# A four-stage scan on VectorE: the first stage's base built from the net term and a slope that holds q, the base and the clamp of p placed anew, and the wait for the base put ahead of the wait for TensorE

## What is computed

```python
def _derivative(q, p, drive, coupling, bias):
    i_couple = jnp.tanh(q) @ coupling.T
    dq = q - q ** 3 / 3.0 - p + drive + i_couple + bias
    dp = EPSILON * (q + ALPHA - BETA * p)
    return (dq, dp)

def _rk4_step(q, p, drive, coupling, bias):
    dq1, dp1 = _derivative(q, p, drive, coupling, bias)
    dq2, dp2 = _derivative(q + 0.5 * DT * dq1, p + 0.5 * DT * dp1, drive, coupling, bias)
    dq3, dp3 = _derivative(q + 0.5 * DT * dq2, p + 0.5 * DT * dp2, drive, coupling, bias)
    dq4, dp4 = _derivative(q + DT * dq3, p + DT * dp3, drive, coupling, bias)
    q_next = q + DT / 6.0 * (dq1 + 2 * dq2 + 2 * dq3 + dq4)
    p_next = p + DT / 6.0 * (dp1 + 2 * dp2 + 2 * dp3 + dp4)
    return (jnp.clip(q_next, -CLAMP, CLAMP), jnp.clip(p_next, -CLAMP, CLAMP))
```

## Time and profile before

| what | value |
|---|---|
| median of 3 runs (lowest, highest) | 5519.89 us (5515.1, 5520.47) |
| the profiled execution: its own time / its span | 5520.96 us / 5519.1 us |
| VectorE busy, share of the span | 4193.2 us, 76% |
| TensorE matmuls busy, share of the span | 4445.0 us, 81% |
| ScalarE / GpSimd busy | 2313.8 us, 42% / 1737.6 us, 31% |
| the scan's 4096 `result` instructions | start from 49.1 to 2927.9 us |

### The profile page before, as it was taken

The page is one execution under the profiler, slowest core; times in us unless marked ns, Lnnn a source line. Parts: engine busy times, 40 slices in busy tenths (PEclk is TensorE's granted clock), DMA queues, the critical chain, the costliest instruction groups (busy, mean ns, idle before and its releaser), DMA issues. The chain is left out here.

```text
span 5519.1 us, 215328 instructions
## 1 busy us (share of the span) xinstructions
PE 4445.0 (81%) x79945; PEld 3846.5 (70%) x79945; DVE 4193.2 (76%) x25970; ACT 2313.8 (42%) x10530; POOL 1737.6 (31%) x5981
## 2 busy tenths in 40 slices
PE   6777777777777777777776788699999999969999
PEld 5666666666666666666665667578777787758777
DVE  8999999999999999999995667377777777631123
ACT  3333333333333333333333556255555555432243
POOL 2444444444444444444443222123323223100000
PEclk5555555555555555555557999699999999989999
DMA  2000000000000000000002000322222222131121
GB/s 70 1 1 1 1 1 1 1 1 1 1 1 1 1 1 1 1 1 1 1 1 78 32 21 17 112 77 66 80 81 88 81 73 65 47 128 55 36 103 39
DMA packets 145850, 188.10 MB, mean 34 GB/s; under 512 B 9373, under 2 KB 75493, under 8 KB 145289
## 3 DMA queue, kind: packets, MB, share of 16 engines
q1 hardware_dynamic: 140800, 182.67, 10.0%
q0 software_dynamic: 624, 0.75, 0.1%
q10 hardware_dynamic: 3992, 0.17, 0.0%
HBM read 143.67 MB, written 39.90 MB: 33 GB/s over the span
## 5 line engine op out<-in xcount | busy, mean ns | idle before, releaser
L211 PE MATMUL bank<-tanh_parts,w_lo 128*128 128x4 f16 x32768 | 1209.3, 169 | 755.5 <-ACT tanh_parts L168 754.3
L211 PEld LDWEIGHTS bank<-tanh_parts,w_lo 128*128 128x128 f16 x32768 | 1034.6, 105 | 940.4 <-ACT tanh_parts L168 939.4
L168 ACT ACTIVATE tanh_parts<-ys 128x8 f16<-128x8 f32 x4096 | 857.4, 209 | 1803.3 <-DVE ys L298 1801.9
L219 PE MATMUL bank<-tanh_parts,w_hi 128*128 128x8 f16 x32768 | 1203.9, 173 | 1.9 <-issue 1.9
L219 PEld LDWEIGHTS bank<-tanh_parts,w_hi 128*128 128x128 f16 x32768 | 1063.0, 104 | 1.9 <-issue 1.9
L298 DVE TENSOR_TENSOR_SCAN ys<-mix,bank 128x24 f32<-128x24 f32 x4096 | 804.4, 201 | 126.3 <-PE bank L219 24.9
L169 ACT ACTIVATE tanh_full<-ys 128x8 f32<-128x8 f32 x4096 | 804.0, 196 | 0.0
L290 DVE TENSOR_TENSOR tanh_parts<-tanh_full,tanh_parts 128x8 f16<-128x8 f32 x4096 | 700.8, 171 | 1.1 <-ACT tanh_full L169 0.5
L1270 POOL TENSOR_TENSOR t_w_qk<-t_raw_qk,t_w_qk 128x512 fp32r<-128x512 f32 x128 | 168.1, 1334 | 765.1 <-ACT t_w_qk L1434 765.1
L475 PE MATMUL t_bank<-t_x,t_w_qk 128*128 128x512 f32 x1536 | 361.5, 391 | 12.8 <-DVE t_x L1690 12.8
L475 PEld LDWEIGHTS t_bank<-t_x,t_w_qk 128*128 128x128 f32 x1536 | 290.0, 189 | 74.0 <-DVE t_x L1690 13.5
(11 more groups left out here) (238 smaller groups left out, 9528.8 us busy)
## 6 DMA issues: line engine op xcount, KB each, us to landing
t_raw_qk<-L_cond_qkv_w_dram SPq DMA_DIRECT2D x128, 256.0 KB, 3.3
t_raw_vo<-L_cond_qkv_w_dram SPq DMA_DIRECT2D x16, 1024.0 KB, 5.2
t_raw_vo<-L_cond_out_w_dram SPq DMA_DIRECT2D x16, 1024.0 KB, 5.2
n<-t_parts SPq DMA_DIRECT2D x14, 1024.0 KB, 6.6
g_raw<-L_cond_ffn_w_dram SPq DMA_DIRECT2D x8, 1024.0 KB, 10.1
g_x<-n SPq DMA_DIRECT2D x8, 1024.0 KB, 8.6
ada_w<-L_cond_ada_w_dram SPq DMA_DIRECT2D x4, 1536.0 KB, 10.8
t_x<-n SPq DMA_DIRECT2D x6, 1024.0 KB, 7.2
```

Of the source, the lines that this page charges most:

```text
L168: act.activation(tanh_parts[:, u, at, :, 0], ys[:, s, at, :, 2], ACT.Tanh, scale=1.0 / SCALE).then_inc(s_th, 1)
L211: pe.matmul(sums[:, :, 2], w_lo[:, w_of, k, m * P:(m + 1) * P], tanh_parts[:, u, k, :, 0], start=(m % 2 == 0 and k == 0), stop=False, skip ...
L219: last = pe.matmul(sums[:, :, 1:3], w_hi[:, w_of, k, m * P:(m + 1) * P], tanh_parts[:, u, k], start=False, stop=(m % 2 == 1 and k == C - 1 ...
```

## The change

In stage 0 the base was GAIN[0] * slope + known, with known = H * net + q. Now the cube is taken with the gain in it and the slope is made as (cub + 1 + GAIN[0]) * q, so that the base is H * net + slope, and `known[0]`, which stage 1 still needs, is made in stage 1. The cube of q is now issued ahead of both `low_part`s. The waits of the first scan on the base and on TensorE change places in stages 0 and 3, and stage 1 gets the wait on the base ahead of TensorE's; stage 2 has none, as before. The clamp of p moves from between the two scans of stage 3 to ahead of the first. In stage 1 `rate[1]` moves from ahead of the `low_part`s to behind the base, and in stages 1 and 2 `twice` and `known[2]` move back by one place. In stage 3 the slope waits for `rate_3`, which stands behind the cube. The number of VectorE's instructions in a step stays 46.

```diff
@@ -295,17 +295,19 @@
                 u, to = s % 2, (s + 1) % STAGES
                 for half, at in enumerate(HALVES):
                     v.wait_ge(s_mm, t * 2 * STAGES + (2 * s + half + 1))
+                    if half == 0 and s != 2:
+                        after("base")
                     v.tensor_tensor_scan(ys[:, to, at].rearrange("p c b n -> p (c b n)"), mix[:, at].rearrange("p c b n -> p (c b n)"),
                                          banks[2 * u + half][:, 0:C // 2 * B * 3], 0.0, ALU.mult, ALU.add).then_inc(s_q, 1)
                     if half == 0 and between is not None:
                         between()
 
-            def cubed(y):
-                own("cub", stt(cub[:, :, :], y, -1.0 / (3.0 * SCALE * SCALE), y, ALU.mult, ALU.mult))
-
-            def sloped(y):
-                after("cub")
-                own("slope", stt(slope[:, :, :], cub[:, :, :], 1.0, y, ALU.add, ALU.mult))
+            def cubed(y, gain=1.0):
+                own("cub", stt(cub[:, :, :], y, -gain / (3.0 * SCALE * SCALE), y, ALU.mult, ALU.mult))
+
+            def sloped(y, of="cub", first=1.0):
+                after(of)
+                own("slope", stt(slope[:, :, :], cub[:, :, :], first, y, ALU.add, ALU.mult))
 
             def based(s, of):
                 own("base", stt(mix[:, :, :, 1], slope[:, :, :], GAIN[s], of))
@@ -315,18 +317,15 @@
             def stage_0(t):
                 v.wait_ge(s_q, t * 2 * STAGES + 2)
                 v.tensor_scalar(q[:, :, :], ys[:, 0, :, :, 2], -CLAMP * SCALE, CLAMP * SCALE, ALU.max, ALU.min).then_inc(s_clip, 1)
+                v.wait_ge(s_clip, t + 1)
+                cubed(q[:, :, :], GAIN[0])
                 low_part(t, 0, 0)
-                v.wait_ge(s_clip, t + 1)
-                cubed(q[:, :, :])
                 low_part(t, 0, 1)
+                sloped(q[:, :, :], first=1.0 + GAIN[0])
                 v.wait_ge(s_net, t + 1)
-                own("known", stt(known[:, 0], net[:, :, :], H, q[:, :, :]))
-                sloped(q[:, :, :])
-                v.wait_ge(s_p, t + 1)
                 stt(rate[:, 0], p[:, :, :], -BETA, q[:, :, :]).then_inc(s_rate, 1)
                 after("slope")
-                based(0, known[:, 0])
-                after("base")
+                own("base", stt(mix[:, :, :, 1], net[:, :, :], H, slope[:, :, :]))
 
                 def between():
                     v.wait_ge(s_rate, t * 3 + 1)
@@ -334,37 +333,35 @@
                 result(t, 0, between)
 
             def stage_1(t):
-                own("known", stt(known[:, 1], rate[:, 0], -EPSILON * H * H, known[:, 0]))
+                own("known_0", stt(known[:, 0], net[:, :, :], H, q[:, :, :]))
                 v.wait_ge(s_q, t * 2 * STAGES + 4)
                 cubed(y1)
-                after("p_1")
-                stt(rate[:, 1], ps_[:, 1], -BETA, y1).then_inc(s_rate, 1)
+                after("known_0")
+                own("known", stt(known[:, 1], rate[:, 0], -EPSILON * H * H, known[:, 0]))
                 low_part(t, 1, 0)
                 sloped(y1)
                 low_part(t, 1, 1)
                 after("slope")
                 based(1, known[:, 1])
+                stt(rate[:, 1], ps_[:, 1], -BETA, y1).then_inc(s_rate, 1)
+                v.wait_ge(s_third, t + 1)
+                own("third_1", stt(thirds[:, 1], y1, THIRD, thirds[:, 0]))
                 v.wait_ge(s_rate, t * 3 + 2)
                 own("p_2", stt(ps_[:, 2], rate[:, 1], EPSILON * H, p[:, :, :]))
-                v.wait_ge(s_third, t + 1)
-                own("third_1", stt(thirds[:, 1], y1, THIRD, thirds[:, 0]))
-                after("base")
-                own("twice", stt(twice[:, :, :], net[:, :, :], 2 * H, q[:, :, :]))
 
                 def between():
-                    after("twice")
-                    own("known", stt(known[:, 2], rate[:, 1], -2 * EPSILON * H * H, twice[:, :, :]))
+                    own("twice", stt(twice[:, :, :], net[:, :, :], 2 * H, q[:, :, :]))
                 result(t, 1, between)
 
             def stage_2(t):
+                after("twice")
+                own("known", stt(known[:, 2], rate[:, 1], -2 * EPSILON * H * H, twice[:, :, :]))
                 v.wait_ge(s_q, t * 2 * STAGES + 6)
                 cubed(y2)
-                after("p_2")
                 stt(rate[:, 2], ps_[:, 2], -BETA, y2).then_inc(s_rate, 1)
                 low_part(t, 2, 0)
                 sloped(y2)
                 low_part(t, 2, 1)
-                after("third_1")
                 own("third_2", stt(thirds[:, 2], y2, 2 * THIRD, thirds[:, 1]))
                 after("slope")
                 based(2, known[:, 2])
@@ -379,21 +376,17 @@
                 cubed(y3)
                 own("rate_3", stt(rate[:, 3], ps_[:, 3], -BETA, y3))
                 low_part(t, 3, 0)
-                sloped(y3)
+                sloped(y3, "rate_3")
                 low_part(t, 3, 1)
-                after("late")
-                own("known", stt(thirds[:, 3], y3, THIRD, known[:, 3]))
+                own("third_3", stt(thirds[:, 3], y3, THIRD, known[:, 3]))
                 v.wait_ge(s_psum, t + 1)
-                after("rate_3")
                 own("moved", stt(p_new[:, :, :], rate[:, 3], EPSILON * H / 3, p_sum[:, :, :]))
-                after("known")
+                after("third_3")
                 based(3, thirds[:, 3])
-                after("base")
-
-                def between():
-                    v.tensor_scalar(p[:, :, :], p_new[:, :, :], (-CLAMP - SHIFT_P) * SCALE, (CLAMP - SHIFT_P) * SCALE,
-                                    ALU.max, ALU.min).then_inc(s_p, 1)
-                result(t, 3, between)
+                after("moved")
+                v.tensor_scalar(p[:, :, :], p_new[:, :, :], (-CLAMP - SHIFT_P) * SCALE, (CLAMP - SHIFT_P) * SCALE,
+                                ALU.max, ALU.min).then_inc(s_p, 1)
+                result(t, 3)
 
             for t in range(T):
                 stage_0(t)
```

## The result

The changed kernel took 5513.53 us (median of 20 runs, 5505.31 to 5520.01), the kernel before 5520.15 us in the same comparison (20 runs, 5515.1 to 5528.01). The ratio is 0.9986, with a 95% interval of 0.9979 to 0.9992: 0.14%, 7 us faster, about a third of the 22 us forecast. The predicted 5498 us lay 16 us too low; the measured time lies inside the wide range and outside the forecast's own.

The account below looks back on a forecast made before the run. The prediction took TensorE's round trip, 1.35 us, as each stage's floor, with separate waits and TensorE holds adding to it. Gains of 0.03 + 0.003 + 0.01 = 0.043 us a step, 22 us, gave 5498 us; own range 5485 to 5510, wide 5464 to 5536.

Parts of the forecast that it names:

- Stage 1: -0.03: Stage 1 falls from 1.38 to 1.35 us, since moving `rate` takes GpSimd's `gp` past both `low_part`s.
- Stage 2: 0: Stage 2 keeps its order in what is timed, so nothing is gained; `twice` and `known` each take another instruction's slot.
- Stage 3: -0.003: Stage 3 gains 0.003 us at the mean: 1.47 us with `rate_3` stretched, 1.41 against 1.42 in other steps.
- all behind it moves by 0.035: In stage 3 the slope, waiting for `rate_3`, goes from 1499.35 to 1499.39, and everything behind it shifts by 0.035 us.
- fixed at 7 in 10: In stage 3, about 7 in 10 steps were taken to have a stretched `rate_3`, worked out from mean durations.
- Stage 0: -0.01: Stage 0 goes from 1.42 to 1.41 us, with the base ending at 1.30 and the scan starting at 1.405.
- I count none: GpSimd's stretches of instructions at their new places in stage 0 were priced at zero, with 0.00 and 0.06 for the range.
- The price of the separate wait: 0.105 behind the base: In stages 3 and 0 a base ending last before its separate wait costs 0.035 to pass and 0.07 more.
- The rival with the full gain: Base's separate wait nearly free in stages 0 and 3: 0.10 us a step, 51 us, 5469 us; chance 2 in 10.
- Nothing is gained: Queue shifts by hundredths; stage 1's 15 us lost to a stretched `p_2` or stage 0's late `low_part`: 5520 us; 1.5 in 10.
- The copy's stretch of the base: GpSimd's trace copy stretches stage 0's base by 0.06: 5526 us, or 5557 with the first `low_part` too; 1.8 in 10.
- VectorE is shut out for the whole GpSimd instruction: Stage 0's first `low_part` waits out GpSimd's product of q; stage takes 1.64 us, kernel 5616 us; 0.2 in 10.

Follow-up runs that it names:

- e2_rate1_only: The kernel before with only stage 1's `rate` (and `p_2` behind it) moved behind the base, `third_1` ahead of `p_2`: 5526.4 us, ratio 1.0.
- repeat: The changed kernel run and profiled once more with no edit: 5516.8 us, ratio 0.9985 to the kernel before.
- e1_slope_free: The changed kernel with stage 3's slope waiting for the cube alone and `rate_3` waited for ahead of the new p: 5495.8 us, ratio 0.9946.
- e1_low_first: The changed kernel with the first `low_part` of stage 0 ahead of the cube again: 5510.1 us, ratio 0.9971.
- e2_swap_only: The kernel before with only the first scan's wait for the base put ahead of TensorE's in stages 0 and 3: 5542.0 us, ratio 1.0028.
- e1_order_back: The changed kernel with the first scan's two waits in stages 0 and 3 in the old order: 5534.9 us, ratio 1.0014.

## Why the prediction was wrong in its size

*Stage 1: -0.03.* Measured -0.025 at the median and -0.023 at the mean, in the way described: `gp` moved from 1496.61 in the earlier trace rows to behind the `low_part`s, which are now unstretched. 1.38 and 1.35 were rounded values of 1.378 and 1.353, and a few long steps took the rest; together 4 us less than forecast. That the gain takes the move of `twice` too was shown by `e2_rate1_only`; the sum has no term for it.

*Stage 2: 0.* The median is unchanged at 1.353; the mean rose by 0.0026 us, 1 us of the kernel. It comes from a few steps, most of them 0.1 to 0.4 us longer than the rest, that stand at the same places in every 128 steps. Over all stages there are 34 of them before and 38 after, and what they take beyond the median of their stage rose from 9.0 to 10.8 us. What these steps wait for wasn't tried.

*Stage 3: -0.003.* The mechanism is as described: the slope waits for `rate_3`, the base comes later and bounds the stage through its separate wait. The step that failed is "all behind it moves by 0.035". In the stretched steps the slope moved by 0.030 (after) and 0.038 (repeat), but the end of the base by 0.045 and 0.052, from 1.329 to 1.374 and 1.381: the second `low_part` starts 0.10 behind a slope that had to wait, where it was 0.09, and `third_3` takes a little longer. So a stretched step takes 1.477 to 1.484 and not 1.47, longer than the 1.469 of before, and one without a meeting 1.415 to 1.418 against 1.422. `e1_slope_free` takes the wait away and gets 0.05 us back in either kind. At the shares of the kernel before, the term would be a loss: +0.004 by the lengths of the profile after (an estimate), and +0.010, 5 us, as measured in the repeat, whose share of 0.73 is nearly that of before. The first profiled execution shows -0.010 only because its share was 0.50, which is luck and nothing that the change did. The share itself was taken as fixed at 7 in 10. It is bounded by three steps in four, which the loop of four fixes, and below that it was 0.50 and 0.73 in two executions of one program.

*Stage 0: -0.01.* This term was mis-sized most: measured +0.0046 us, so 7 us of the missing gain, in either execution. The step that failed is "I count none", of GpSimd's stretches at the new places. The first `low_part`, which I saw coming 0.05 behind the product of q, was stretched: the pair takes 0.27 us from 1500.02, where 0.08 and 0.16 would make 0.24. The slope, which had taken 0.20 beside the product of net in the earlier trace rows and which I set at 0.17, took 0.19, again behind that product (1500.15 and 1500.21). In `e1_low_first`, where both stand elsewhere, they take 0.17 us each. The base ended 1.32 to 1.33 behind the first scan instead of 1.30. A second error went the other way: I set the second scan 0.22 behind the first, and it came at 0.18 to 0.19, because in stage 3 the base bounds the first scan and not the second. TensorE's hold of 0.04 us was as forecast.

*The price of the separate wait: 0.105 behind the base.* Right, seen in the profile after and in `e2_swap_only`, which is slower by what it says. The rival with the full gain is refuted. What I had not seen is that a delay of the first scan of stage 3 costs nothing in stage 0: the old order of the waits should cost 0.035 us in each of the two stages, and `e1_order_back` loses 0.033 in stage 3 and none in stage 0.

*The rivals.* "Nothing is gained" comes nearest to what was measured, and 0.14% is within the 0.2% that was given a chance of 1.9 in 10. Of its two reasons one came true, the late first `low_part` of stage 0 that costs more than worked out; stage 1 kept its gain. The copy's stretch of the base didn't happen in the changed kernel, and by luck: GpSimd's two products before it began 0.03 us earlier than worked out and took 0.22 us each instead of 0.26 and 0.24, so the copy started 1.03 behind the first scan and not 1.12, 0.11 ahead of the base. It did happen as soon as the base was 0.06 us earlier (`e1_low_first`). That VectorE is shut out for the whole GpSimd instruction is refuted at every place: the stretches are 0.02 to 0.07 us. This is the rule of the Trainium skill, page SBUF — State Buffer, section Who interferes with whom; the trace agrees that the two engines hold each other up, but not with the whole length, and not that the one that starts first goes free: the copy starts 0.01 us ahead of `rate_3` in both kinds of meeting, and in 123 of 379 it is the copy that is stretched.

The sum at a share of 0.73 is -0.006 us a step, 3 us; at 0.50 it is -0.025, 13 us; the median's 7 us lies between. Of the forecast's 0.043 us a step, 0.037 are missing in the repeat: 0.015 in stage 0, 0.013 in stage 3, 0.006 in stage 1 and 0.003 in stage 2.

## What to carry to other kernels

When an instruction needs two waits, put in front, as its own instruction, the one that is over well before the other, and work out the end of both with the 0.10 us that belongs to the separate one and the 0.04 that belongs to the carried one. A wait put in front of one instruction delays the end of the chain by more than the wait itself: 0.03 to 0.04 us at the slope was 0.05 at the base. Follow the loop over more than one stage before a delay is counted: here the next stage hung on the second scan, and a delay of the first cost it nothing. In a loop of instructions of 0.17 us, moving one by 0.05 us changes which instructions meet another engine's; list every such meeting at the new places and price it at both ends, because in stage 0 these meetings, not the waits, decided the sign of the term. And before a share of steps is taken as a rate of chance, look which steps they are: here a quarter of them were fixed by another engine's loop.

## What the runs showed of the hardware

- Whether VectorE or GpSimd is held up where two of their instructions start about 0.01 us apart isn't fixed: with `rate_3` 0.01 us behind the copy, either `rate_3` takes 0.23 and the copy 0.20, or 0.17 and 0.25. Where they meet, the first kind was 256 of 379 and 375 of 379 in two executions of the same kernel, and 88 of 379 in one of a kernel that differs from it in another stage. It makes some 7 of the 10 us between the two profiled executions of the changed kernel, 5511.1 and 5520.9 us. What decides it wasn't found.
- A TENSOR_SCALAR with one fp32 input in SBUF (the clamp of q) is stretched too, 0.24 us against 0.17, when a GpSimd instruction with two inputs starts 0.01 us ahead of it. The scans, which read one input from PSUM, were never seen longer than 0.205 us.
- A wait that stands as its own instruction costs 0.07 us more than one that the instruction carries, whether it waits for TensorE or for VectorE itself: 0.10 against 0.035 from the end of what is waited for.
